# Third FFN stage: the up part is rounded by GpSimd, in place and with an added constant, instead of by ScalarE

## The chip, the cores and the metric

One core of one Trainium2 chip. The metric is the device time of one execution in microseconds, the median of the runs. Engines: TensorE (PE; PEld is its weight load), VectorE (DVE), ScalarE (ACT), GpSimd (POOL) and SyncE (SP), which only issues DMAs here.

## What is computed

Two layers of cross attention and FFN over x (4 x 1024 tokens, 256 wide), each with a residual. The change lies in the FFN of the first layer, which imitates 16-bit integers:

```python
def act_qdq(x):
    qmax = 2.0 ** (ACT_BITS - 1) - 1.0
    scale = jnp.maximum(jnp.max(jnp.abs(x)) / qmax, 1e-12)
    return jnp.clip(jnp.round(x / scale), -qmax - 1.0, qmax) * scale
x = act_qdq(x)
up = act_qdq(x @ lpbq_dequant(w_up).T)
gate = act_qdq(x @ lpbq_dequant(w_gate).T)
sig = fixed_qdq_u16(jax.nn.sigmoid(gate))
gate = act_qdq(gate * sig)
o = act_qdq(gate * up)
return o @ lpbq_dequant(w_down).T
```

Each act_qdq needs the largest absolute value of the whole tensor before it can round a single element. That is what cuts the FFN into stages.

## The kernel before

The program runs attention 0, the FFN, attention 1 and a mixture of experts one after the other. The function ffn is written as four blocks; between two blocks all engines meet. Inside a block each engine runs its own list of instructions in the order written, and counters (semaphores) hold it back.

The gate and the up part have 4096 x 768 values each. They are handled as NU = 24 units of 128 partitions x UW = 1024 columns. G holds all 24 units of the gate in SBUF; the up part has no room there and goes through DRAM (up_scratch), unit by unit.

The second block (lines 1690 to 1784) makes the up part and the gate times its sigmoid. In it GpSimd already runs two tensor_scalar per unit on f_sg (L1754, L1757: cap the sigmoid, then round it by adding GRID), and VectorE a scalar_tensor_tensor that takes GRID off and multiplies with an int16 tile (L1767), then two reduces (L1770, L1773). At its end SyncE issues the loads of the first four up units into ul[0..3] (L1504, called from load), and VectorE computes the scales ksl and kup, one value a partition, in SBUF.

The third block (from line 1786) is the one changed. Per unit u:

- ScalarE rounds the gate unit to int16, gq = round(G x ksl) (L1792), after product u-2 has freed that buffer (s_pr), and counts s_g3; then it waits for the load of the unit (s_ul) and rounds the up unit, uq = round(ul x kup) (L1794), and counts s_uq. gq and uq have two buffers each, ul has four.
- SyncE waits for s_uq of unit u-4 and issues the load of unit u into the same ul buffer (L1801, L1504).
- VectorE waits for s_g3 and s_uq, multiplies gq and uq into G (L1815) and counts s_pr; then it takes the largest absolute value of the unit before (L1819), one column of am3. These are products and reduces in the order product 0, product 1, reduce 0, product 2, reduce 1, and so on.
- TensorE only helps to spread the maximum over the partitions at the end (L1536, L1546). GpSimd has nothing to do.

After the last reduce, VectorE folds the 24 columns (L1823), the maximum is spread, and the fourth block starts: ScalarE rounds G again and TensorE multiplies with the down weights (L1882).

Of the kernel before, what the change touches and what calls it, by code (L numbers as in the profile page):

```python
# [9 lines left out]
I16 = mybir.dt.int16  # L10
U16 = mybir.dt.uint16
U8 = mybir.dt.uint8
ACT = mybir.ActivationFunctionType
AX = mybir.AxisListType
RMAX = bass.bass_isa.ReduceOp.max

P = 128
# [66 lines left out]
def pipeline(eng, body, first, last, lo, hi):  # L84

    for t in range(first, lo):
        body(At(t))
    with eng.Fori(0, (hi - lo + 1) // 2) as i:
        body(At(lo, i))
        body(At(lo + 1, i))  # L90
    for t in range(hi + 1, last + 1):
        body(At(t))
# [49 lines left out]
def _program(nc, stack, x, ctx_kv, mask, w, out):  # L142
# [32 lines left out]
    att0.close()  # L175
    old, sem = sem, Sems(nc)
    ffn(nc, sem, old, sbuf, xs, dict(fw, ident=ident, hmean=hmean, hrstd=hrstd, hamax=hamax, early=early))
    until_ffn.close()
    old, sem = sem, Sems(nc)
# [1223 lines left out]
def ffn(nc, sem, retired, sbuf, xs, c):  # L1403
# [12 lines left out]
    NU, UW = 24, 1024  # L1416
    UC = NU // NCH
    QM = 32767.0
    U16S = 65536.0
    GRID = 128.0  # L1420

    def s(n):
        return sem("f_" + n)
# [6 lines left out]
    s_ul, s_uq, s_g3, s_pr, s_am3 = [s(f"ul{i}") for i in range(4)], s("uq"), s("g3"), s("pr"), s("am3")  # L1430
# [4 lines left out]
    with ExitStack() as st:  # L1435
# [7 lines left out]
        am3 = sbuf(st, "am3", [P, NU])  # L1443
# [25 lines left out]
        r1, r2, r3 = Region(hold), Region(hold), Region(hold)  # L1469
# [8 lines left out]
        ul_at = r2.at  # L1478
        bh, bl = [[r2(f"f_b{v}{i}", [P, KT, CW], F32R) for i in range(2)] for v in "hl"]
        gq = [r3(f"f_gq{i}", [P, UW], I16) for i in range(2)]  # L1480
        uq = [r3(f"f_uq{i}", [P, UW], I16) for i in range(2)]
        assert r3.at <= ul_at
        r3.at = ul_at
        ul = [r3(f"f_ul{i}", [P, UW]) for i in range(4)]
# [5 lines left out]
        def unit(n):  # L1490
            return G[:, bass.ds(n * UW, UW)]
# [4 lines left out]
        def load_h(sp, t):  # L1496
            for i, h_ in enumerate((bh, bl)):
                sp.wait_ge(s_hs[t.p], t.of(lambda n: 32 * (n // 2 + 1)))
                sp.dma_start(h_[t.p][:].rearrange("p k n -> p (k n)").bitcast(F32),
                             hscr[bass.ds(t.n * 2 + i, 1)].rearrange("u p n -> p (u n)")  # L1500
                             ).then_inc(s_b[t.p], 16)

        def load(sp, t):
            sp.dma_start(ul[t.t0 % 4][:], uscr[bass.ds(t.n, 1)].rearrange("u p n -> p (u n)")  # L1504
                         ).then_inc(s_ul[t.t0 % 4], 16)
# [13 lines left out]
        def link(dve, instruction):  # L1519

            instruction.then_inc(s_sc, 1)
            links[0] += 1
            dve.wait_ge(s_sc, links[0])

        def integer_scale(dve, k, unit_scale, extra, scale, factor):

            dve.wait_ge(s_all, k + 1)
            link(dve, dve.tensor_scalar(tmp, ps[k % 2][:, 0:1], unit_scale, extra / QM, ALU.mult, ALU.mult))
            link(dve, dve.tensor_scalar(scale, tmp, 1e-12, None, ALU.max))
            link(dve, dve.reciprocal(tmp, scale))  # L1530
            link(dve, dve.tensor_scalar(factor, tmp, unit_scale, extra, ALU.mult, ALU.mult))

        def rows_max(pe, k):

            pe.wait_ge(s_loc, k + 1)
            pe.transpose(ps[6 + k % 2][0:1, 0:P], loc[:, k:k + 1], c["ident"][:]).then_inc(s_row, 1)  # L1536

        def fold_max(dve, k):
            dve.wait_ge(s_row, k + 1)
            dve.tensor_reduce(gmax[0:1, k:k + 1], ps[6 + k % 2][0:1, 0:P], AX.X, ALU.max).then_inc(s_gm, 1)  # L1540
            dve.wait_ge(s_gm, k + 1)
            dve.tensor_copy(grow[:, k % 2, :], gmax[0:1, k:k + 1].broadcast_to([1, P])).then_inc(s_bc, 1)

        def spread_max(pe, k):
            pe.wait_ge(s_bc, k + 1)
            pe.transpose(ps[k % 2][:, 0:1], grow[:, k % 2, :], c["ident"][0:1, 0:1]).then_inc(s_all, 1)  # L1546


        with nc.Block() as block:
            @block.sync  # L1550
            def _(sp):
                retired.clear(sp)

                def store(t):
                    for i, (h_, ready) in enumerate(((hh, s_hh), (hl, s_hl))):
                        sp.wait_ge(ready, t.of(lambda n: 2 * n + 2))
                        sp.dma_start(hscr[bass.ds(t.n * 2 + i, 1)].rearrange("u p n -> p (u n)"),
                                     h_[t.p][:].rearrange("p k n -> p (k n)").bitcast(F32)).then_inc(s_hs[t.p], 16)
                pipeline(sp, store, 0, NCH - 1, 2, 5)
                for i in range(2):  # L1560
                    load_h(sp, At(i))
                for i in range(2):
                    sp.wait_ge(s_hs[i], 32 * NCH // 2)
# [126 lines left out]
        with nc.Block() as block:  # L1690
# [58 lines left out]
            def _(pool):  # L1749
                def body(t):  # L1750
                    for q in range(UC):
# [4 lines left out]

                        pool.tensor_scalar(v, v, 1.0, GRID, ALU.mult, ALU.add).then_inc(s_su, 1)  # L1757
                for t in range(NCH):
# [3 lines left out]
            def _(dve):  # L1762
                def body(t):
                    for q in range(UC):
                        par = (t.t0 + q) % 2
                        dve.wait_ge(s_su, t.of(lambda n: UC * n + q + 1))
                        dve.scalar_tensor_tensor(unit(t.n * UC + q), sg[par][:], GRID, iq[q][:], ALU.subtract,  # L1767
                                                 ALU.mult).then_inc(s_g2, 1)
# [17 lines left out]
        with nc.Block() as block:  # L1786
            @block.scalar
            def _(act):
                def ints(t):
                    if t.t0 >= 2:  # L1790
                        act.wait_ge(s_pr, t.of(lambda n: n - 1))
                    act.activation(gq[t.p][:], unit(t.n), ACT.Copy, scale=ksl).then_inc(s_g3, 1)  # L1792
                    act.wait_ge(s_ul[t.t0 % 4], 16 * (t.t0 // 4 + 1))
                    act.activation(uq[t.p][:], ul[t.t0 % 4][:], ACT.Copy, scale=kup).then_inc(s_uq, 1)  # L1794
                for t in range(NU):
                    ints(At(t))

            @block.sync
            def _(sp):
                for t in range(4, NU):  # L1800
                    sp.wait_ge(s_uq, t - 3)  # L1801
                    load(sp, At(t))

            @block.tensor
            def _(pe):
                rows_max(pe, 4)
                spread_max(pe, 4)

            @block.vector
            def _(dve):  # L1810
                def body(t):
                    if t.t0 < NU:
                        dve.wait_ge(s_g3, t.of(lambda n: n + 1))
                        dve.wait_ge(s_uq, t.of(lambda n: n + 1))
                        dve.tensor_tensor(unit(t.n), gq[t.p][:], uq[t.p][:], ALU.mult).then_inc(s_pr, 1)  # L1815
                    a = t + -1
                    if a.t0 >= 0:
                        dve.wait_ge(s_pr, a.of(lambda n: n + 1))
                        dve.tensor_reduce(am3[:, bass.ds(a.n, 1)], unit(a.n), AX.X, ALU.max,  # L1819
                                          apply_absolute_value=True).then_inc(s_am3, 1)  # L1820
                pipeline(dve, body, 0, NU, 2, NU - 1)
                dve.wait_ge(s_am3, NU)
                dve.tensor_reduce(loc[:, 4:5], am3[:], AX.X, ALU.max).then_inc(s_loc, 1)  # L1823
                fold_max(dve, 4)
                link(dve, dve.tensor_tensor(sps, ssl, sup, ALU.mult))
                integer_scale(dve, 4, sps, 1.0, spr, kpr)
# [356 lines left out]
```

## Time and profile before

| | us |
|---|---|
| median of 3 runs (lowest, highest) | 1242.75 (1242.65, 1244.66) |
| profiled execution | 1243.19 |
| its span, first to last instruction | 1241.5 |
| third FFN block, first ScalarE operation to last reduce's end | 479.40 to 536.99 |
| busy share of TensorE, VectorE, ScalarE, GpSimd | 86%, 77%, 50%, 35% |

The span leaves out what lies around the instructions, 1.7 us here. In the timeline a row gives start, duration, engine, line, operation, output <- inputs; in brackets stands how long the engine was idle before it and who released it. The records of two VectorE operations in a row overlap by some 0.08 us, so the pace is read from their starts.

### The profile page before, as it was taken

Reading aid. Unit: us, or ns where it says so; the run is one execution under the profiler, and the core shown is the slowest. Engines: PE = TensorE matmul, PEld = TensorE weight load, DVE = VectorE, ACT = ScalarE, POOL = GpSimd, SP = SyncE. Lnnn points to the kernel's source line nnn. Section 1 sums busy time; section 2 is a strip of 40 time slices with the busy share of each in tenths; the row PEclk is TensorE's granted clock in tenths of the full one; section 3 lists DMA queues with packets and bytes.
Section 4 is the critical chain, followed back from the end, with each engine's and each line's share of the span. In section 5 each row is a group of like instructions: output and inputs, shape, how many; then the busy total and the mean of one; then the engine's idle time right before and its main releaser. Section 6 shows DMA issues by size and latency. Waiting matters only on the chain. (4 is left out here: it accounts for less than half of the span.)

```text
span 1241.5 us, 21565 instructions
## 1 busy us (share of the span) xinstructions
PE 1071.5 (86%) x6208; PEld 894.9 (72%) x6208; DVE 953.8 (77%) x2589; ACT 620.0 (50%) x1335; POOL 429.0 (35%) x514
## 2 busy tenths in 40 slices
PE   7999999996998980049986799999999969999998
PEld 5777777875886660049943698889888958777776
DVE  4688998885775998966453778887788758888886
ACT  1566777763556996967445233333333323332333
POOL 1245444441002881000011244455544533434333
PEclk9999999997999995569999899999999979999999
DMA  8000000000234766703123400101000000000000
GB/s 266 1 2 1 1 1 2 2 1 34 102 133 157 271 220 214 226 1 92 41 61 108 155 1 0 42 0 42 0 0 0 1 1 9 26 17 17 25 17 26
DMA packets 35551, 71.87 MB, mean 58 GB/s; under 512 B 3531, under 2 KB 23071, under 8 KB 35295
## 3 DMA queue, kind: packets, MB, share of 16 engines
q1 hardware_dynamic: 34111, 70.28, 17.0%
q10 hardware_dynamic: 1376, 0.79, 0.3%
q8 instruction: 33, 0.54, 0.2%
q14 instruction: 31, 0.25, 0.1%
HBM read 40.41 MB, written 30.65 MB: 57 GB/s over the span
## 5 line engine op out<-in xcount | busy, mean ns | idle before, releaser
L1068 PE MATMUL a_ps<-VW,a_PT 128*128 (+1 forms) x640 | 143.7, 380 | 0.0
L1068 PEld LDWEIGHTS a_ps<-VW,a_PT 128*128 128x128 f32 x640 | 119.5, 190 | 15.1
L1106 ACT ACTIVATE a_U<-a_U 128x1280 f32<-128x1280 f32 x32 | 40.7, 1270 | 112.5 <-DVE a_U L1179 112.5
L1085 ACT COPY a_PT<-a_ps 128x512 f32<-128x512 f32 (+1 forms) x96 | 46.0, 518 | 90.3 <-PE a_ps L1031 90.3
L1171 DVE TENSOR_REDUCE a_mx<-a_ps 128x4 f32<-128x320 f32 x128 | 62.3, 486 | 33.4 <-PE a_ps L1017 33.2
L1942 PE MATMUL m_ps<-m_wh,m_xh 128*128 128x512 f32 x256 | 87.1, 422 | 0.0
L2040 POOL TENSOR_TENSOR m_half<-m_half 128x512 f32<-128x512 f32 x32 | 41.0, 1283 | 132.3 <-ACT m_half L2002 132.3
L854 DVE TENSOR_SCALAR a_U<-a_ps 128x320 f32<-128x320 f32 x128 | 59.2, 483 | 32.9 <-PE a_ps L662 22.9
L1942 PE MATMUL m_ps<-m_wh,m_xl 128*128 128x512 f32 x256 | 82.1, 402 | 0.0
L1942 PE MATMUL m_ps<-m_wl,m_xh 128*128 128x512 f32 x256 | 81.4, 400 | 0.0
L745 PEld LDWEIGHTS a_ps<-vals,a_PT 128*128 128x128 f32 x640 | 76.4, 192 | 2.0 <-issue 0.4
L1017 PE MATMUL a_ps<-keysh,a_xnT 128*128 (+1 forms) x256 | 68.1, 347 | 10.8 <-DVE a_U L1179 9.3
L1123 POOL TENSOR_TENSOR a_U<-a_U,a_rc 128x1280 f32<-128x1280 f32 x32 | 74.6, 2332 | 7.3 <-DVE a_rc L1158 7.3
L745 PE MATMUL a_ps<-vals,a_PT 128*128 128x34 f32 (+1 forms) x640 | 74.2, 273 | 0.0
L2074 DVE SCALAR_TENSOR_TENSOR xs<-m_ps,m_g,xs 128x256 f32 (+1 forms) x128 | 61.2, 478 | 13.2 <-PE m_ps L1942 10.6
L2009 ACT ACTIVATE m_ex<-m_ls 128x8 f32<-128x8 f32 x32 | 6.7, 209 | 129.5 <-DVE m_ls L2095 129.5
L804 ACT ACTIVATE a_U<-a_U,a_mx 128x80 f32<-128x80 f32 x256 | 67.6, 346 | 0.0
L1536 PE MATMUL f_ps<-ident,loc 128*1 128x128 f32 x5 | 1.6, 362 | 75.4 <-DVE loc L1823 59.7
L1116 POOL TENSOR_TENSOR a_xrs<-a_xve,mhalf 128x1 f32<-128x1 f32 x32 | 17.5, 548 | 138.0 <-DVE a_xve L1227 138.0
L1754 POOL TENSOR_SCALAR f_sg<-f_sg 128x1024 f32<-128x1024 f32 x24 | 28.5, 1186 | 103.4 <-ACT f_sg L1718 103.3
L825 POOL TENSOR_TENSOR a_U<-a_U,a_mx 128x320 f32<-128x320 f32 x64 | 45.8, 718 | 46.4 <-DVE a_mx L859 46.0
L1179 DVE TENSOR_TENSOR a_U<-a_ps,a_mx 128x320 f32<-128x320 f32 x128 | 59.5, 486 | 2.2
(252 smaller groups left out, 3134.7 us busy)
## 6 DMA issues: line engine op xcount, KB each, us to landing
up_scratch<-f_ub SPq DMA_DIRECT2D x24, 512.0 KB, 2.9
f_ul<-up_scratch SPq DMA_DIRECT2D x24, 512.0 KB, 4.4
vw_scratch<-vw_stage SPq DMA_DIRECT2D x8, 640.0 KB, 4.2
VW<-vw_scratch SPq DMA_DIRECT2D x4, 1280.0 KB, 5.8
xs<-in_x SPq DMA_DIRECT2D x4, 1024.0 KB, 12.2
h_scratch<-f_hh SPq DMA_DIRECT2D x8, 512.0 KB, 2.6
h_scratch<-f_hl SPq DMA_DIRECT2D x8, 512.0 KB, 3.1
f_bh<-h_scratch SPq DMA_DIRECT2D x8, 512.0 KB, 4.5
```

The costliest lines, as they stand in the source:

```text
L745: last = pe.matmul(PV[:, h0 * E0:(h0 + nh) * E0], PTs[t.p][:, j, :], pr.vals[:].rearrange("p b s e -> p (b s e)")[:, bass.ds(t.batch * (NS ...
L804: last = act.activation(v, v, ACT.Exp, bias=mx[nxt.p][:, h:h + 1])
L825: pool.tensor_tensor(v, v, mx[a.p][:, 4 * g:4 * g + 4].unsqueeze(2).broadcast_to([P, 4, KP]), ALU.add).then_inc(s_sh, 1)
L854: dve.tensor_scalar(U[a.p][:, g * QW:(g + 1) * QW], S[sb[g]][:, 0:QW], CLAMP, -CLAMP, ALU.min, ALU.max).then_inc(s_clip, 1)
L1017: last = pe.matmul(S[sb[g]][:, 0:QW], x_[a.p][:, k, :], c[k_][:].rearrange("p b m n -> p (b m n)")[:, bass.ds(a.batch * (KT * SW) + k * SW ...
L1068: last = pe.matmul(Y[:, 0:D], PTs[t.p][:, j, :], c["VW"][:].rearrange("p b j d -> p (b j d)")[:, bass.ds(t.batch % 2 * (NJ * D) + j * D, D ...
L1085: act.copy(PTs[t.p][:, js[0]:js[-1] + 1, :].rearrange("p j n -> p (j n)"), R[k][:, 0:len(js) * P]).then_inc(s_PTe, 1)
L1123: pool.tensor_tensor(heads(U[a.p]), heads(U[a.p]), rc[a.p][:].unsqueeze(2).broadcast_to([P, H, KP]), ALU.mult).then_inc(s_N, 1)
L1171: dve.tensor_reduce(mx[a.p][:, 4 * g:4 * g + 4], quad(g), AX.X, ALU.max).then_inc(s_mx, 1)
L1179: dve.tensor_tensor(U[a.p][:, g * QW:(g + 1) * QW].rearrange("p (h k) -> p h k", k=KP), quad(g), mx[a.p][:, 4 * g:4 * g + 4].unsqueeze(2). ...
L1942: last = pe.matmul(o_, x_[a.p][:, k, :], w_[:, k, cols], start=(n == 0), stop=(n == 3 * KT - 1))
L2074: dve.scalar_tensor_tensor(xt(t), X[e // 2][:, (e % 2) * D:(e % 2 + 1) * D], g[t.p][:, e:e + 1], xt(t), ALU.mult, ALU.add).then_inc(s_acc, 1)
```

## The change

ScalarE's second operation and the tiles uq go. GpSimd gets a list of its own in the third block: as soon as a load has landed, it computes ul x kup + 12582912 in place. That number is 1.5 x 2^23; a float32 of that size has no fraction bits, so the sum is rounded to a whole number. VectorE's product becomes a scalar_tensor_tensor that subtracts the constant from ul and multiplies with gq. As ul is now read last by the product, the load that refills it waits for s_pr instead of s_uq. VectorE's loop over pairs of units is written out.

```diff
+    ROUND = 12582912.0
-        uq = [r3(f"f_uq{i}", [P, UW], I16) for i in range(2)]
@@ third block, scalar
-                def ints(t):
-                    if t.t0 >= 2:
-                        act.wait_ge(s_pr, t.of(lambda n: n - 1))
-                    act.activation(gq[t.p][:], unit(t.n), ACT.Copy, scale=ksl).then_inc(s_g3, 1)
-                    act.wait_ge(s_ul[t.t0 % 4], 16 * (t.t0 // 4 + 1))
-                    act.activation(uq[t.p][:], ul[t.t0 % 4][:], ACT.Copy, scale=kup).then_inc(s_uq, 1)
-                for t in range(NU):
-                    ints(At(t))
+                for u in range(NU):
+                    if u >= 2:
+                        act.wait_ge(s_pr, u - 1)
+                    act.activation(gq[u % 2][:], unit(u), ACT.Copy, scale=ksl).then_inc(s_g3, 1)
+
+            @block.gpsimd
+            def _(pool):
+                for u in range(NU):
+                    v = ul[u % 4][:]
+                    pool.wait_ge(s_ul[u % 4], 16 * (u // 4 + 1))
+                    pool.tensor_scalar(v, v, kup, ROUND, ALU.mult, ALU.add).then_inc(s_uq, 1)
 
             @block.sync
             def _(sp):
-                for t in range(4, NU):
-                    sp.wait_ge(s_uq, t - 3)
-                    load(sp, At(t))
+                for u in range(4, NU):
+                    sp.wait_ge(s_pr, u - 3)
+                    load(sp, At(u))
@@ vector
-                def body(t):
-                    if t.t0 < NU:
-                        dve.wait_ge(s_g3, t.of(lambda n: n + 1))
-                        dve.wait_ge(s_uq, t.of(lambda n: n + 1))
-                        dve.tensor_tensor(unit(t.n), gq[t.p][:], uq[t.p][:], ALU.mult).then_inc(s_pr, 1)
-                    a = t + -1
-                    if a.t0 >= 0:
-                        dve.wait_ge(s_pr, a.of(lambda n: n + 1))
-                        dve.tensor_reduce(am3[:, bass.ds(a.n, 1)], unit(a.n), AX.X, ALU.max,
-                                          apply_absolute_value=True).then_inc(s_am3, 1)
-                pipeline(dve, body, 0, NU, 2, NU - 1)
+                def largest(u):
+                    dve.wait_ge(s_pr, u + 1)
+                    dve.tensor_reduce(am3[:, u:u + 1], unit(u), AX.X, ALU.max,
+                                      apply_absolute_value=True).then_inc(s_am3, 1)
+
+                for u in range(NU):
+                    dve.wait_ge(s_g3, u + 1)
+                    dve.wait_ge(s_uq, u + 1)
+                    dve.scalar_tensor_tensor(unit(u), ul[u % 4][:], ROUND, gq[u % 2][:], ALU.subtract,
+                                             ALU.mult).then_inc(s_pr, 1)
+                    if u >= 1:
+                        largest(u - 1)
+                largest(NU - 1)
```

## Rows read from the trace of the kernel before

**Rows 1.** The page: the span in 40 slices, busy tenths of two engines.
```profile
DVE  4688998885775998966453778887788758888886
...
POOL 1245444441002881000011244455544533434333
```

**Rows 2.** Window of the third FFN stage: busy us of PE, PEld, DVE, ACT, POOL; clock, DMA.
```profile
489.00:495.00 6.00, 0.00 (x0) 0.00 (x0) 6.00 (x6) 5.98 (x6) 0.00 (x0) 0.50 0.81 249
```

**Rows 3.** Groups by line and form, 481 to 540 us: busy, mean ns | idle before.
```profile
L1794 ACT ACTIVATE f_uq<-f_ul,sc 128x1024 int16<-128x1024 f32 x24 | 27.2, 1132 | 0.0
```

**Rows 4.** Timeline of the stage's head: start, duration, engine, line, operation.
```profile
479.40 1.15 ACT L1792 ACTIVATE f_gq<-G,sc 128x1024 int16<-128x1024 f32 x1 [10.49 <-PEq L1690]
480.46 1.13 ACT L1794 ACTIVATE f_uq<-f_ul,sc 128x1024 int16<-128x1024 f32 x1
481.50 1.13 ACT L1792 ACTIVATE f_gq<-G,sc 128x1024 int16<-128x1024 f32 x1
481.62 6.56 SPq L1504 DMA_DIRECT2D f_ul<-up_scratch  x4
481.70 1.23 DVE L1815 TENSOR_TENSOR G<-f_gq,f_uq 128x1024 f32<-128x1024 int16 x1 [2.80 <-ACT f_uq L1794]
...
483.78 1.23 DVE L1815 TENSOR_TENSOR G<-f_gq,f_uq 128x1024 f32<-128x1024 int16 x1 [0.85 <-ACT f_uq L1794]
...
486.05 1.22 DVE L1815 TENSOR_TENSOR G<-f_gq,f_uq 128x1024 int16 x1
...
487.18 1.21 DVE L1819 TENSOR_REDUCE am<-G  x1
```

**Rows 5.** Timeline of the stage's end.
```profile
534.66 2.33 DVE L1819 TENSOR_REDUCE am<-G  x2
```

**Rows 6.** Timeline of the second FFN stage, its start.
```profile
388.65 1.04 POOL L1754 TENSOR_SCALAR f_sg<-f_sg 128x1024 f32<-128x1024 f32 x1 [90.44 <-ACT f_sg L1718]
...
389.78 1.06 POOL L1757 TENSOR_SCALAR f_sg<-f_sg 128x1024 f32<-128x1024 f32 x1
...
399.37 1.21 DVE L1767 SCALAR_TENSOR_TENSOR G<-f_sg,f_iq 128x1024 f32<-128x1024 f32 x1
...
400.50 1.21 DVE L1770 TENSOR_REDUCE amu<-f_ub 128x1 f32<-128x1024 f32 x1
```

**Rows 7.** Timeline of the second FFN stage, GpSimd and VectorE meeting.
```profile
412.97 1.23 DVE L1767 SCALAR_TENSOR_TENSOR G<-f_sg,f_iq 128x1024 f32 x1
413.05 2.04 POOL L1754 TENSOR_SCALAR f_sg<-f_sg 128x1024 f32<-128x1024 f32 x1 [0.26 <-ACT f_sg L1718]
...
414.11 1.21 DVE L1770 TENSOR_REDUCE amu<-f_ub 128x1024 f32 x1
...
416.30 1.04 POOL L1754 TENSOR_SCALAR f_sg<-f_sg 128x1024 f32<-128x1024 f32 x1
416.39 2.03 DVE L1767 SCALAR_TENSOR_TENSOR G<-f_sg,f_iq 128x1024 f32 x1
...
418.34 1.21 DVE L1770 TENSOR_REDUCE amu<-f_ub 128x1024 f32 x1
...
443.58 1.20 DVE L1773 TENSOR_REDUCE am<-G  x1
...
443.85 1.04 POOL L1754 TENSOR_SCALAR f_sg<-f_sg 128x1024 f32<-128x1024 f32 x1 [0.42 <-ACT f_sg L1718]
```

**Rows 8.** Groups by line: a two-input operation of GpSimd.
```profile
L2040 POOL TENSOR_TENSOR m_half<-m_half 128x512 f32<-128x512 f32 x32 | 41.0, 1283 | 132.3 <-ACT m_half L2002 132.3
```

**Rows 9.** The up loads, issue to landing: first four, next eight, last twelve.
```profile
L1504 SPq DMA_DIRECT2D f_ul<-up_scratch x4: 362/452/782, 469.4 to 471.1; - x4
...
DMA to landing us min/median/max: 4.6/6.1/7.0
...
DMA to landing us min/median/max: 3.5/4.2/4.4
...
DMA to landing us min/median/max: 4.0/4.4/4.5
```

## The prediction

> **What bounds the kernel now.** The page comes first: in the 17th of its 40 slices (496.6 to 527.6 us), wholly inside the third FFN stage and the only part the change touches, VectorE's digit is 9 and GpSimd's is 0 [rows 1]. The table of windows over that stage shows VectorE busy 6.00 of the 6 us from 489 to 495, ScalarE 5.98, GpSimd 0.00, and the DMA engines 0.81 [rows 2]. The reader is to see two engines that are both nearly full, and only one of them without a gap. One rounding of the up part takes ScalarE 1.13 us [rows 3], a product 1.22 and a reduce 1.21 us [rows 4]. VectorE's records overlap a little, so I take its pace from starts in the timeline: product 486.05, reduce 487.18, that is 1.13 us each and 2.26 us a unit [rows 4]. ScalarE, left alone, went from one gate rounding to the next in 2.10 us (479.40 to 481.50) [rows 4]. So VectorE bounds this stage from its second product (483.78) on, ScalarE only the head of it: product 0 waits until 481.70 for two roundings in a row, and product 1 sat idle 0.85 us for the next two [rows 4]. The last reduce ends at 536.99 [rows 5]. Check: 483.78 + 47 operations x 1.13 = 536.9.
>
> **What is removed.** 24 roundings of the up part on ScalarE, 24 x 1.13 = 27.2 us [rows 3]. They lie beside VectorE's work, so past the head their removal is worth nothing: VectorE is late next, and already was.
>
> **What stays as it is.** The product becomes a scalar_tensor_tensor with one float32 and one int16 input instead of two int16 inputs. The second stage has just that form (L1767): product 399.37, next operation 400.50, again 1.13 us [rows 6]. Cost 0.00 a unit, and below nothing it cannot go, since the reduces beside it show the same 1.13 us for 1024 columns [rows 4]. VectorE's loop becomes straight code; the loop's registers ran beside its work without a gap, so nothing. ScalarE's rounding of the gate now waits for product u-2 only; it has a whole cycle in hand.
>
> **What is added.** 24 tensor_scalar on GpSimd, in place, float32. The same shape with two immediate numbers takes 1.04 us when nothing hinders it (388.65, and 443.85) [rows 6, 7]. Here one of the two numbers is a column in SBUF (kup), and no GpSimd row shows that. The lower bound is 1.04; the upper one is a full second input: 1.28 us for 512 columns of two inputs makes up to 2.6 for 1024 [rows 8]. I take 1.04, because one value a partition is nearest to an immediate, and keep the upper half for a rival. At 1.04 in a cycle of 2.26 GpSimd itself is no bound.
>
> **What the two engines do to each other.** The second stage shows it in both directions. At 413.05 a GpSimd operation begins 0.08 us after a VectorE product; it lasts 2.04 instead of 1.04 and ends at 415.09, 0.98 us after VectorE's next operation began (414.11) [rows 7]. At 416.30 GpSimd is first by 0.09 us: the product of 416.39 lasts 2.03 instead of 1.21 and the next VectorE operation begins at 418.34, 1.00 us after GpSimd's end at 417.34, where an unhindered one comes 1.13 after its product's start [rows 7]. So a product held up behaves as if it had started 0.13 us before GpSimd ended, and GpSimd held up as if it started 0.06 us before the next VectorE operation. A reduce disturbs nobody: 443.58 reduce 1.20 us, 443.85 GpSimd 1.04 us, together [rows 7]. The product and GpSimd exclude each other, whoever is first; the reduce leaves 1.13 us in which GpSimd's 1.04 just fits.
> The Trainium skill ("SBUF — State Buffer", the list under its two sides of ports) has this as a rule that speaks against the change: GpSimd and a VectorE instruction with two SBUF inputs share one port pair as an exclusive lock, held for the whole instruction by whoever starts first. The trace agrees (2.04 and 2.03 us) [rows 7]. By the rule the head of the stage gains 0.4 us as below; without it, 2.0.
>
> **The head, step by step.** The stage's first ScalarE operation starts at 479.40 [rows 4]; GpSimd may start there too, since four loads were issued from 469.4 on and landed within 7.0 us at most [rows 9]. GpSimd unit 0: 479.40 to 480.44; unit 1 from 480.53 (0.09 later, as 388.65 + 1.04 to 389.78 [rows 6]) to 481.57. Product 0 wants to start at 480.66 (gate rounding to 480.55, plus the 0.11 seen from 481.59 to 481.70 [rows 4]), finds GpSimd 0.13 us ahead, and counts from 481.57 - 0.13 = 481.44. GpSimd unit 2 then gets the pair at 482.51 and ends at 483.55; product 1 counts from 483.42, reduce 0 comes at 484.55, product 2 at 485.68. Before, product 2 started at 486.05 [rows 4]. If product 1 went ahead of unit 2 instead, unit 3 would begin just ahead of product 2 and the same 485.68 would result. Gain: 486.05 - 485.68 = 0.37 us.
>
> **The loads, which are moved.** The refill of a slot was released by ScalarE's rounding of unit u and is now released by product u, its last reader; SyncE has nothing else queued. Steady, the refill goes out 1.21 + 0.03 = 1.24 us after the product's start (0.03: 481.59 to 481.62 [rows 4]), lands L later, and GpSimd starts, say, 0.11 after that, as VectorE did behind ScalarE [rows 4]. L was 4.0 to 4.5 us, median 4.4, for the last twelve loads and 3.5 to 4.4 for the eight before [rows 9]. GpSimd then ends 1.24 + 4.4 + 0.11 + 1.04 = 6.79 us after the product of four units earlier, against 4 x 2.26 = 9.04: the data are never late. But the end must also not fall past the start of the product of three units later by more than 0.13: with T for the cycle, 3T is at least L + 1.24 + 0.11 + 1.04 - 0.13 = L + 2.26. At L = 4.4, T = 2.22; at 4.5, 2.25; VectorE's 2.26 still decides, by a margin of 0.02 us in L (4.52). In other words GpSimd starts 1.1 to 1.3 us into the cycle, just behind the product.
>
> **Sum.** Span 1241.5 - 0.4 = 1241.1. The profiled execution took 1243.19, 1.7 outside the span, so 1242.8; it stood 0.4 above the median of 1242.75, hence 1242.4 us.
>
> **Rivals.**
> *A, slower: loads land later and GpSimd gets in front of the products.* Place: the reduce's slot, units 4 to 23. It decides from L = 4.52 us. At L = 5.0, T = 2.42, and 20 units x 0.16 = 3.2 us give 1245.6; at 5.5, T = 2.59 and 20 x 0.33 = 6.6 give 1249.0; past 5.52 the load lands behind the start of a product and the cost is gone. For it: the margin is 0.02 us, and the first four loads took 4.6 to 7.0 [rows 9]. Against it: those were issued within 2 us of each other, the spaced ones stayed at 4.5 or less, and a delay lengthens the cycle and so corrects two thirds of itself. Were there no such correction, each product could lose 2.03 - 1.21 = 0.82 us, 20 us in all. The Trainium skill ("GPSIMD Engine Reference", Key points) warns of just this, contention between GpSimd and VectorE instructions with two SBUF inputs; how often it strikes here no run shows yet. Chance 0.12.
> *B, slower: GpSimd pays for the scalar from SBUF.* Up to 1.3 us fits; at 1.9 a cycle is 1.9 + 1.13 - 0.06 - 0.13 = 2.84, and 23 units x 0.58 = 13 us give 1256. For it, only that no row shows the form. Chance 0.04.
> *C, faster by more than forecast: no blocking at the head.* Product 0 at 480.66, product 1 at 481.79, product 2 at 484.05 instead of 486.05: 2.0 us off, 1240.7. For it: GpSimd might begin a little late, so that product 0 comes first. Against: 416.30, where 0.09 us of lead decided [rows 7]. Chance 0.08.
> *D, the change does not do what it says:* GpSimd runs ahead at every unit and ScalarE was never the bound, so nothing moves: 1242.75. That is within my own case and not counted apart. Anything else, 0.02.
>
> **How the numbers follow.** My case, 1241.9 to 1243.5, has 0.74. A measurement of this kernel can tell about 0.2%, that is 2.5 us. Faster by more than that (under 1240.3) only the lucky end of C: 0.03. Slower (over 1245.2): A from L = 5.0 on, B and some of the rest, 0.13. Within: 0.84. The range: 1240.4 takes in C, 1247.0 takes in A up to about L = 5.2; B and the far end of A stay outside.
>
> **What would show it.** Product 2 at about 485.7 on the old time line; product starts 2.26 apart; GpSimd records starting 0.2 to 1.3 us after a product's start, lasting 1.04 to 2.0; product records of 1.21 to 1.27. Wrong would be: product records over 1.4 us again and again and starts 2.35 or more apart (A), GpSimd records that last over 1.3 us during a reduce (B), idle time of VectorE before products with a DMA or GpSimd named.

## The result, and the profile after

| | before | after |
|---|---|---|
| median, us | 1242.75 | 1240.13 |
| profiled execution; its span | 1243.19; 1241.5 | 1241.62; 1239.9 |
| third FFN block, first ScalarE operation to last reduce's end | 479.40 to 536.99 (57.59) | 480.62 to 538.22 (57.60) |
| mixture of experts, first to last record of its most frequent matmul line (L1942; after L1947) | 1019.1 to 1234.8 (215.7) | 1020.3 to 1233.2 (212.9) |

The ratio is 0.9979, interval 0.9970 to 0.9988: 2.6 us faster, 0.21%. Forecast were 1242.4 us and no measurable change; the range ended at 1240.4, so the time lies just below it. One of the 17 executions of after took 2728.09 us, in a slow state; the ratio leaves it out, and no trace of it was kept.

The table says where the time is. Everything ahead of the changed block, which the change doesn't touch, took 1.2 us longer in the profiled execution after. Single executions differ by that much and more: before ranged from 1239.91 to 1245.15 us. The changed block took as long as before. From its end to the mixture of experts both need 482.1 us, and from the start of the last matmul of L1942 (after: L1947) to the end of the span 6.7 us. The mixture of experts alone is 2.8 us shorter. 1.2 - 2.8 = -1.6, which is the difference of the spans. The whole gain lies in a stage that begins 482 us later and whose code the change leaves as it was, but for line numbers that are 5 higher.

The page after: two engines in 40 slices, as in [rows 1].

```profile
DVE  4798998884775999976554778888788758888886
...
POOL 1344445440002885410011245444554443334333
```

GpSimd's 17th slice has gone from 0 to 4, VectorE's stays 9 [rows 1]. The window of the changed stage, columns as in [rows 2]:

```profile
490.00:496.00 6.00, 0.00 (x0) 0.00 (x0) 6.00 (x7) 3.33 (x3) 3.91 (x3) 0.50 0.73 231
```

VectorE is as full as before, 6.00 of 6 us, ScalarE is down from 5.98 to 3.33. The groups of the stage after, columns as in [rows 3]:

```profile
L1799 POOL TENSOR_SCALAR f_ul<-f_ul,sc 128x1024 f32<-128x1024 f32 x24 | 31.0, 1293 | 29.4 <-DMA f_ul<-up_scratch 20.9 <-POOLq L1690 8.5
L1822 DVE SCALAR_TENSOR_TENSOR G<-f_ul,f_gq 128x1024 f32<-128x1024 f32 x24 | 30.9, 1292 | 1.8 <-POOL f_ul L1799 1.8
```

The head of the stage after, the timeline that answers to [rows 4]:

```profile
480.62 2.19 ACT L1792 ACTIVATE f_gq<-G,sc 128x1024 int16<-128x1024 f32 x2 [10.49 <-PEq L1690]
480.65 6.42 POOL L1799 TENSOR_SCALAR f_ul<-f_ul,sc 128x1024 f32<-128x1024 f32 x4 [8.45 <-POOLq L1690]
481.88 3.19 DVE L1822 SCALAR_TENSOR_TENSOR G<-f_ul,f_gq 128x1024 f32<-128x1024 f32 x2 [1.77 <-POOL f_ul L1799]
...
485.00 1.21 DVE L1816 TENSOR_REDUCE am<-G 128x1 f32<-128x1024 f32 x1
486.13 2.02 DVE L1822 SCALAR_TENSOR_TENSOR G<-f_ul,f_gq 128x1024 f32<-128x1024 f32 x1
...
488.07 1.21 DVE L1816 TENSOR_REDUCE am<-G 128x1 f32<-128x1024 f32 x1
```

GpSimd gets into its second unit ahead of product 0 and holds it back; product 1 follows at once, ahead of GpSimd's third unit (two products in 3.19 us), and product 2, held back by GpSimd's unit 3, lasts 2.02 us. Reduce 1 starts 7.45 us after the stage's first operation; before it was 487.18 - 479.40 = 7.78 [rows 4]. That is 0.33 us gained. It is lost again in the middle:

```profile
506.45 1.12 POOL L1799 TENSOR_SCALAR f_ul<-f_ul,sc 128x1024 f32<-128x1024 f32 x1 [1.37 <-DMA f_ul<-up_scratch]
507.29 1.35 DVE L1822 SCALAR_TENSOR_TENSOR G<-f_ul,f_gq 128x1024 f32<-128x1024 f32 x1
...
508.79 1.12 POOL L1799 TENSOR_SCALAR f_ul<-f_ul,sc 128x1024 f32<-128x1024 f32 x1 [1.22 <-DMA f_ul<-up_scratch]
509.69 1.29 DVE L1822 SCALAR_TENSOR_TENSOR G<-f_ul,f_gq 128x1024 f32<-128x1024 f32 x1
```

GpSimd's 506.45 operation starts when its load lands, 1.42 us into the cycle of 505.03, and ends 0.28 us into the product at 507.29, which then lasts 1.35 instead of 1.21 us. Four products of the stage have this (1.35, 1.29, 1.29, 1.25), and their cycles are 2.40, 2.34, 2.35 and 2.30 instead of 2.26: 0.14 + 0.08 + 0.09 + 0.04 = 0.35 us.

Then the mixture of experts. The chain of work that ended last there (start, us, what), of before:

```profile
1120.15 1.42 PE m_ps L1942 x6
...
1121.70 0.22 DVE m_ls L2095
...
1123.05 0.21 DVE m_sel L2112
...
1123.47 0.24 DVE m_g L2119
...
1124.13 0.44 DVE m_xl L2132
...
1124.61 0.61 PE m_ps L1970 x4
```

The same stretch of after:

```profile
1120.06 2.80 PE m_ps L1947 x12
1122.86 0.12 PE m_ps L2000
1122.98 1.41 PE m_ps L1947 x6
1124.39 0.50 PE m_ps L1975 x4
```

Before, the chain leaves TensorE for 3 us and runs through VectorE's routing of the experts, and so it does in each of the twelve turns; after, it never leaves TensorE. The fourth part of the page says the same in one line: PE 14%, DVE 2% and issue 1% of the span before, PE 17% and DVE 0% after. So here VectorE was on the path, by a small margin, with TensorE nearly full at the same time. Windows of 120 us inside this stage, columns as in [rows 2], first before, then after (TensorE has gone from 118.83 us to all 120.00, so little more is to be had here from VectorE):

```profile
1080.00:1200.00 120.00, 118.83 (x574) 95.09 (x573) 104.64 (x450) 40.24 (x144) 45.65 (x54) 1.00 0.06 20
```

```profile
1080.00:1200.00 120.00, 120.00 (x586) 96.80 (x584) 106.46 (x456) 41.11 (x144) 46.21 (x56) 1.00 0.06 20
```

The stage is a loop, and a turn handles two tiles of tokens. A turn, from one loop branch of VectorE to the next, took 13.38 us before and 13.17 after (medians of the 11 stretches between 12 branches). Where VectorE's turn got shorter is seen in its timeline at two places. Before:

```profile
1132.62 0.15 DVE L2152 TENSOR_SCALAR m_ve<-m_ag 128x1 f32<-128x1 f32 x1
1133.38 0.48 DVE L2074 SCALAR_TENSOR_TENSOR xs<-m_ps,m_g,xs 128x256 f32 x1 [0.60 <-PE m_ps L1942]
...
1136.40 0.23 DVE L2112 SCALAR_TENSOR_TENSOR m_sel<-m_iota,m_fi,m_sel 128x8 f32<-128x8 f32 x1
1136.85 0.23 DVE L2119 SCALAR_TENSOR_TENSOR m_g<-m_ex,m_rs,m_sel 128x8 f32<-128x8 f32 x1 [0.22 <-DVE m_sel L2112]
```

After:

```profile
1132.32 0.15 DVE L2157 TENSOR_SCALAR m_ve<-m_ag 128x1 f32<-128x1 f32 x1
1132.95 0.48 DVE L2079 SCALAR_TENSOR_TENSOR xs<-m_ps,m_g,xs 128x256 f32 x1 [0.48 <-PE m_ps L1947]
...
1135.97 0.23 DVE L2117 SCALAR_TENSOR_TENSOR m_sel<-m_iota,m_fi,m_sel 128x8 f32<-128x8 f32 x1
1136.32 0.23 DVE L2124 SCALAR_TENSOR_TENSOR m_g<-m_ex,m_rs,m_sel 128x8 f32<-128x8 f32 x1
```

Between the first two rows lies the loop's branch. From the start of the one to the start of the other it was 0.76 us, and is 0.63; I call it the way back. Between the other two lie only register and semaphore instructions: 0.45 us before, 0.35 after; I call it the halt. Together 1.21 and 0.98 us, and 0.23 is what a turn lost, within 0.02. From the first branch to the last it was 147.3 us before (1065.7 to 1213.0) and 144.8 after (1066.6 to 1211.4), 2.5 less. In the first turn, ahead of the first branch, the halt was 0.71 us before (1055.71 to 1056.42) and 0.35 after (1056.97 to 1057.32), 0.36 more. The two account for the stage's 2.8 us. The idle time of the way back is put down to TensorE in both, but nothing in TensorE's list changed between them. The sequencer's own records of the branch say more (first and last start us). Before:

```profile
L88 DVEq COMPARE_BRANCH  x1: 56/56/56, 1132.7 to 1132.7; - x1
L88 DVEq FUSED_REGOPS  x1: 63/63/63, 1133.0 to 1133.0; - x1
```

After:

```profile
L88 DVEq COMPARE_BRANCH  x1: 56/56/56, 1132.4 to 1132.4; - x1
L88 DVEq FUSED_REGOPS  x1: 63/63/63, 1132.6 to 1132.6; - x1
```

The branch itself takes 0.056 us in both; the loop's first instruction started 0.31 us after the branch did before, and 0.19 after. That instruction sets registers and waits for no semaphore, so no other engine can have held it up: the delay is in VectorE's own list of instructions.

### The profile page after: what moved, and what is told of

Its sections match the earlier page's. It is cut to its first block and busy times, and to the rows that moved or that the text cites. A ratio compares the mean times of both kernels' runs of the same rounds, so it can differ in the third digit from the quotient of the medians.

```text
span 1239.9 us, 21476 instructions
## 1 busy us (share of the span) xinstructions
PE 1070.6 (86%) x6208; PEld 895.1 (72%) x6208; DVE 959.2 (77%) x2589; ACT 596.8 (48%) x1311; POOL 459.6 (37%) x538
## 5 line engine op out<-in xcount | busy, mean ns | idle before, releaser
L1947 PE MATMUL m_ps<-m_wh,m_xh 128*128 128x512 f32 x256 | 87.2, 422 | 0.0
L1947 PE MATMUL m_ps<-m_wh,m_xl 128*128 128x512 f32 x256 | 82.0, 402 | 0.0
L1947 PE MATMUL m_ps<-m_wl,m_xh 128*128 128x512 f32 x256 | 81.4, 399 | 0.0
L745 PEld LDWEIGHTS a_ps<-vals,a_PT 128*128 128x128 f32 x640 | 79.5, 198 | 2.2 <-issue 0.4
L745 PE MATMUL a_ps<-vals,a_PT 128*128 128x34 f32 (+1 forms) x640 | 77.2, 279 | 0.0
L1116 POOL TENSOR_TENSOR a_xrs<-a_xve,mhalf 128x1 f32<-128x1 f32 x32 | 17.5, 548 | 135.5 <-DVE a_xve L1227 135.5
L817 POOL TENSOR_TENSOR a_xrs<-a_xve,mhalf 128x1 f32<-128x1 f32 x32 | 21.4, 669 | 114.3 <-DVE a_xve L928 114.3
```

Source lines behind the costliest of these rows:

```text
L745: last = pe.matmul(PV[:, h0 * E0:(h0 + nh) * E0], PTs[t.p][:, j, :], pr.vals[:].rearrange("p b s e -> p (b s e)")[:, bass.ds(t.batch * (NS ...
L1947: last = pe.matmul(o_, x_[a.p][:, k, :], w_[:, k, cols], start=(n == 0), stop=(n == 3 * KT - 1))
```

## The experiments

What could make a loop shorter whose code is unchanged? Either what the three engines do in the third block (ScalarE's list 24 instructions shorter, GpSimd's longer), or the removed loop of VectorE, or only where VectorE's instructions lie: writing the loop out makes VectorE's program 51 instructions longer ahead of the mixture of experts. Eleven kernels tell these apart, and a twelfth tests the rule for GpSimd. The first four do one thing each. The number 51 comes from the loop: its 14 instructions and one ahead of it did two units a turn, and written out the same 22 units take 66, 3 a unit. The expectation of e_unroll counts the loop's growth as 30 rows, and e_dve30 was made after that count, so it is not the same shift as e_unroll.

**e_unroll.** Before, with VectorE's loop of the third block written out, and nothing else.
```diff
-                pipeline(dve, body, 0, NU, 2, NU - 1)
+                for t in range(NU + 1):
+                    body(At(t))
```


> The kernel before with one part of the change: VectorE's loop of the third FFN stage written out, so that its program ahead of the mixture-of-experts loop is 30 rows longer (1586 instead of 1556 ahead of that loop's branch). Theory 1 (the gain of the changed kernel comes from where VectorE's code lies): about 1240.2 us, 2.6 below the kernel before, and 13.17 us instead of 13.38 for a pair of tiles in the mixture-of-experts loop; the third FFN stage stays at 57.6 us. Theory 2 (ScalarE's 24 fewer rows) and theory 3 (GpSimd's 26 more rows): 1242.7 and 13.38. Theory 4 (the gain lies in the third FFN stage after all): 1242.7.

Measured: 1239.35 us against 1242.02, ratio 0.9977 (0.9968 to 0.9986); a turn 13.17 us. This one edit gives all of the gain (0.9979). ScalarE's roundings are all there, GpSimd has nothing to do, and the third block takes 57.60 us (481.60 to 539.20), as in both other kernels.

**e_pool26.** Before, with 26 small GpSimd operations in the third block.
```diff
+            @block.gpsimd
+            def _(pool):
+                for i in range(26):
+                    pool.memset(amt[:, i:i + 1], 0.0)
```


> The kernel before with 26 one-column memsets added to GpSimd's list in the third FFN stage, where it has nothing to do. Theory 3 (GpSimd's longer program moves its later loops): about 1240.2 us and 13.17 us for a pair of tiles. Theories 1, 2 and 4: 1242.7 and 13.38.

Measured: 1242.27 us, ratio 1.0000 (0.9989 to 1.0011), a turn 13.38. The length of GpSimd's list has no part in it.

**e_act24.** After, with ScalarE's 24 instructions put back as copies of one column.
```diff
                     act.activation(gq[u % 2][:], unit(u), ACT.Copy, scale=ksl).then_inc(s_g3, 1)
+                    act.copy(sc[:, 13 + u % 8:14 + u % 8], sh)
```


> The changed kernel with 24 one-column copies added to ScalarE's list, one behind each gate rounding of the third FFN stage, where it then has about 1.1 us to spare; its program is as long again as in the kernel before. Theory 2 (ScalarE's shorter program): back to 1242.7 us and 13.38 us for a pair of tiles. Theories 1, 3 and 4: 1240.1 and 13.17; the third FFN stage itself stays at 57.6 us.

Measured: 1240.14 us, ratio to before 0.9980 (0.9968 to 0.9991), a turn 13.16. The gain stays with ScalarE's list as long as before, so its length has no part in it either.

**e_dve30.** Before, with 30 copies of one column at the head of VectorE's fourth block, where it waits for ScalarE anyway. This moves all that follows by 30 instructions and leaves the loop of the third block.
```diff
             def _(dve):
+                for i in range(30):
+                    dve.tensor_copy(amt[:, i:i + 1], sh)
+
                 def body(t):
```


> The kernel before with 30 one-column copies added to VectorE's list at the head of the fourth FFN stage, where it waits 2.8 us for ScalarE's first rounding; they write a scratch column each that nobody reads. Theory 1 (place of VectorE's code): about 1240.2 us and 13.17 us for a pair of tiles, as if the loop had been written out, or up to 0.5 more if the copies last longer than the wait. Theories 2, 3 and 4: 1242.7 and 13.38.

Measured: 1242.62 us against 1242.02, ratio 1.0003 (0.9994 to 1.0012), a turn 13.38. No gain, against what the expectation had for a mere shift. The copies were no cost that could hide it: they end ahead of the first product of the block.

```profile
536.47 2.12 DVE L1838 COPY amt<-sc 128x1 f32<-128x1 f32 x30 [0.52 <-PEq L1786]
538.78 1.22 DVE L1848 TENSOR_TENSOR wTl<-f_oq,wTh 128x1024 fp32r<-128x1024 int16 x1 [0.19 <-ACT wTh L1868]
```

Its timeline has something new, though. Same two places as above:

```profile
1129.00 0.15 DVE L2155 TENSOR_SCALAR m_ve<-m_ag 128x1 f32<-128x1 f32 x1
1129.85 0.48 DVE L2077 SCALAR_TENSOR_TENSOR xs<-m_ps,m_g,xs 128x256 f32 x1 [0.70 <-PE m_ps L1945]
...
1132.88 0.23 DVE L2115 SCALAR_TENSOR_TENSOR m_sel<-m_iota,m_fi,m_sel 128x8 f32<-128x8 f32 x1
1133.23 0.23 DVE L2122 SCALAR_TENSOR_TENSOR m_g<-m_ex,m_rs,m_sel 128x8 f32<-128x8 f32 x1
```

The halt is down to 0.35 us as in after, but the way back is 0.85 us instead of 0.76. The extra tenth hasn't gone; it has moved from the 32nd record of the loop's body to the 2nd, 30 places forward. So it doesn't seem to belong to an instruction, but to a place in VectorE's program.

**e_dve1, e_dve2, e_dve3 and e_aft1.** The same copies, one, two and three ahead of the unchanged loop, and one in after.

> The kernel before with one single one-column copy added at the head of VectorE's list for the fourth FFN stage, where it waits for ScalarE anyway. So far: writing the loop out makes VectorE's program 51 instructions longer and the mixture-of-experts loop faster, 30 more copies leave it as it was. Theory 1a (what counts is whether the loop ahead lies at an odd or an even place): about 1240 us, 13.16 us for a pair of tiles, and 0.19 instead of 0.31 us from the loop's branch to VectorE's next instruction. Theory 1b (a coarser grain than two instructions): some other value between 13.16 and 13.38, or 13.38. Theory 5 (not the place but the missing loop in the third FFN stage makes the later one faster): 1242.4 and 13.38.

> The same with two copies. Theory 1a: 13.38 us for a pair of tiles and 0.31 us behind the branch, as with none. Theory 1b: some other value. Theory 5: 13.38.

> The same with three copies, so that the place is as far from that of the kernel before as 51 is when counted in steps of four. Theory 1a: 13.16 us for a pair of tiles and 0.19 us behind the branch. Theory 1b with a grain of four: 13.16 here, and another value with one copy. Theory 5: 13.38.

> The changed kernel with one one-column copy added at the head of VectorE's list for the fourth FFN stage. Theory 1a: the gain is lost, 1242.5 us, 13.38 us for a pair of tiles and 0.31 us behind the branch, although all of the change is there. Theory 1b: between 1240.1 and 1242.5. Theory 5: 1240.1 and 13.16.

Measured: e_dve1 1244.46 us against 1243.81, ratio 1.0007 (0.9997 to 1.0017), a turn 13.33; e_dve2 13.33 and e_dve3 13.29 (one execution each, 1240.96 and 1241.08 us, so that only their turns are used); e_aft1 1239.71 us, ratio 0.9964 (0.9951 to 0.9978), a turn 13.17. Whether the shift is odd or even makes no difference, and three copies don't give what 51 give, so a step of four is out too. With one copy the halt is at the 31st record, with two at the 30th. With three copies the halt is down to 0.35 and the way back still 0.76. What is left of the theories: the way back is long as long as such a place lies inside the loop, and short once it has left the loop at its head, after some 32 instructions.

**e_dve36, e_dve51 and e_unroll13.** 36 and 51 copies ahead of the unchanged loop of before, and 13 copies on top of e_unroll, 64 in all.

> The kernel before with 36 one-column copies at the head of VectorE's list for the fourth FFN stage. A short halt inside the mixture-of-experts loop's first pass sat at VectorE's record 32 without padding, 31 with one copy, and near record 2 with thirty: it looks like an edge at a fixed place of VectorE's program over which the loop is shifted. Theory 6 (a loop's way back costs 0.31 us when such an edge lies in its first part, and 0.19 when not): 36 copies push the edge ahead of the loop, so 0.19 us behind the branch, about 13.16 us for a pair of tiles, and some 2.5 us off the total, 0.2 of it lost again because 36 copies last a little longer than the wait that hides them. Theory 5 (the missing loop in the third FFN stage is what counts, not the place): 0.31, 13.33 and the total of the kernel before.

> The same with 51 copies, so that the mixture-of-experts loop lies exactly where it lies with the third stage's loop written out. Theory 6: 0.19 us behind its branch and 13.16 us for a pair of tiles; attention 1's loop gets 0.27 instead of 0.19 us behind its branch, as in the changed kernel; the fourth stage begins up to 1.0 us late. Theory 5: 0.31 and 13.38, and 0.19 in attention 1.

> The kernel before with VectorE's loop of the third stage written out (51 instructions) and 13 one-column copies at the head of the fourth: 64 in all. Theory 6 with edges every 64 instructions: the halt is back at record 32, 0.31 us behind the branch, 13.38 us for a pair of tiles. Theory 6 with edges farther apart (128 or more), or theory 5: 0.19 and 13.16.

Measured: e_dve36 1239.47 us against 1242.26, ratio 0.9980 (0.9967 to 0.9992). That is the gain of the change from 36 useless instructions and nothing of the change. Its rows around the branch (the way back is 0.63 us; the halt's stretch is 0.34):

```profile
1129.45 0.15 DVE L2155 TENSOR_SCALAR m_ve<-m_ag 128x1 f32<-128x1 f32 x1
1130.08 0.48 DVE L2077 SCALAR_TENSOR_TENSOR xs<-m_ps,m_g,xs 128x256 f32 x1 [0.48 <-PE m_ps L1945]
```

That also rules out the missing loop as the cause, as the loop is there. e_dve51 and e_unroll13 ran once each (1240.81 and 1239.84 us); their turns are in the table. In e_unroll13 neither the halt nor the long way back has returned, against the first of the two theories in its expectation. All kernels by their shift, medians over the turns:

| VectorE instructions more than before | kernel | way back + halt, us | turn, us | attention 1, behind the branch, us |
|---|---|---|---|---|
| 0 | before, e_pool26 | 0.76 + 0.45 = 1.21 | 13.38 | 0.19 |
| 1 and 2 | e_dve1, e_dve2 | 0.76 + 0.41 = 1.17 | 13.33 | 0.19 |
| 3 | e_dve3 | 0.76 + 0.35 = 1.11 | 13.29 | 0.19 |
| 30 | e_dve30 | 0.86 + 0.35 = 1.21 | 13.38 | 0.19 |
| 36 | e_dve36 | 0.63 + 0.35 = 0.98 | 13.16 | 0.19 |
| 51 | e_dve51, e_unroll, after, e_act24, e_gpdelay | 0.63 + 0.35 = 0.98 | 13.16 to 13.17 | 0.27 |
| 52 | e_aft1 | 0.63 + 0.35 = 0.98 | 13.17 | 0.27 |
| 64 | e_unroll13 | 0.62 + 0.35 = 0.97 | 13.14 | 0.27 |

The turn less the two stretches is 12.16 to 12.19 us in every row: what VectorE saves there is what the stage saves. The last column is the same effect in another loop, VectorE's in attention 1, and goes the other way: at 51 and more its first instruction comes 0.27 us after the branch instead of 0.19. There a turn takes 19.27 to 19.28 us in all of them, so it costs nothing. e_dve51 keeps the loop of the third block and has the same pair of values as the four kernels in which it is written out; what they share is the number 51.

**e_gpdelay.** The other half of the prediction is the rule by which GpSimd gets in front of the products. After, with GpSimd held back by a memset (320 columns, 0.36 us) ahead of each rounding.
```diff
+                    pool.memset(gd[:], 0.0).then_inc(s_gd, 1)
+                    pool.wait_ge(s_gd, u + 1)
                     pool.tensor_scalar(v, v, kup, ROUND, ALU.mult, ALU.add).then_inc(s_uq, 1)
```


> The changed kernel with a 320-column memset of GpSimd (0.37 us) and a wait for it between each load's landing and the rounding, so that each rounding starts some 0.42 us later. If the prediction's rule for the third stage holds (three cycles are at least load time plus 1.24 + 0.08 + 1.12 - 0.13, here plus 0.42), a cycle takes (4.4 + 2.31 + 0.42) / 3 = 2.38 instead of 2.26 us, the stage 59.5 instead of 57.6 and the kernel 2 us more than the changed one. If GpSimd does not hold the products up, both stay as they are, as 0.42 us are small beside the two cycles of reserve that the data have.

Measured: 1243.83 us against 1242.26, ratio 1.0003 (0.9991 to 1.0015; the two medians alone would give 1.0013). By the ratios that is about 3 us more than after, which stands at 0.9979 to its own before. The third block takes 59.8 us (480.46 to 540.22) instead of 57.6, which is 2.2 of them; the rest is within the two intervals. The turn of the mixture of experts stays at 13.16. Its timeline:

```profile
491.24 0.36 POOL L1800 MEMSET f_gd<- 128x320 f32 x1
491.40 1.23 DVE L1825 SCALAR_TENSOR_TENSOR G<-f_ul,f_gq 128x1024 f32<-128x1024 f32 x1
491.69 1.91 POOL L1802 TENSOR_SCALAR f_ul<-f_ul,sc 128x1024 f32<-128x1024 f32 x1
492.54 1.21 DVE L1819 TENSOR_REDUCE am<-G 128x1 f32<-128x1024 f32 x1
...
493.71 1.23 DVE L1825 SCALAR_TENSOR_TENSOR G<-f_ul,f_gq 128x1024 f32<-128x1024 f32 x1
```

Products start 2.31 us apart. The stage's loss is near what was expected (2.2 against 1.9 us); the way to it is partly another. For the first dozen units the loads are no longer what times GpSimd: it starts 0.29 us behind a product, is held until that ends, lasts 1.91 us, and the next memset and the wait behind it bring the next rounding to 2.32 us after this one (491.69 and 494.01): its own chain is the cycle. Later single products are held too (one takes 2.10 us). So a GpSimd with 1.12 + 0.36 us of work a unit is already the bound of this stage, though that is far from filling the cycle of 2.26: a rounding that starts under a product is held until the product ends and takes 1.91 us.

## Why the prediction was wrong

**The head, a gain of 0.37 us.** Right: 0.33, with product 1 ahead of unit 2, which the prediction named as the other order with the same end. GpSimd's rounding takes 1.12 us (506.45), not the 1.04 of [rows 6]. That row caps the sigmoid; the one at 389.78, which multiplies and adds as the new one does, takes 1.06, so that 0.06 us are left for the scalar from SBUF. Rival B would have needed over 1.3.

**The product's new form, nothing.** Right: 1.21 us, and starts 2.26 or 2.27 us apart in 16 of the 20 cycles from 489.20 on.

**The exclusion of product and GpSimd.** Right (held products last 2.06 and 2.02 us, against 2.03 in [rows 7]), and so C, which needed its absence, did not occur: that the time is near C's 1240.7 is an accident.

**The loads and the rule 3T ≥ L + 2.26.** The mechanism was right, the size off by the same 0.08 us of the rounding and by loads whose times vary: with 1.12 the point from which it decides is L = 4.44 instead of 4.52, and the stage's loads have a median of 4.4 us. So it decided now and then, four times, for 0.35 us in all. The prediction gave rival A from L = 5.0 on, at 3.2 us; a tenth of that came. How often it decides differs between executions: e_aft1, with the same third block, has cycles of 2.30 us at most.

**The sum over the third block.** 0.33 gained and 0.35 lost is nothing, where 0.37 was forecast as gain. For this block it is rival D, that nothing moves, though for another reason.

**The step that failed** is the sentence "VectorE's loop becomes straight code; the loop's registers ran beside its work without a gap, so nothing". It is right for the loop that was written out, and it was asked of that loop alone. Writing it out made the program longer by 51 instructions and moved every later loop of VectorE. e_unroll shows that this by itself gives a ratio of 0.9977, against 0.9979 for the whole change, and e_dve36 (0.9980) that not even the loop has to go. The other mistake made this one possible: the views were read for the changed block alone. The chain of waits of before, read over the mixture of experts, passes through VectorE in every turn, and a tenth of a microsecond in it counts twelve times. With that chain in hand, a change that alters the number of VectorE's instructions is no longer safe to put at nothing, and 0.84 for no change was too much. But its size, some 2.8 us, is known from these runs alone. Nothing in the trace of before says on which side of such a place the loop would come to lie; before was at the slow end of the table, and from a kernel at its fast end the same edit could have led to the slow one.

**What is shown and what isn't.** Shown: the gain comes from the place of VectorE's instructions, and the two stretches account for it. Not shown: what kind of memory has its border at that place. The DMA queues that carry instructions, in the trace of before, 1050 to 1062 us:

```profile
q8 instruction: 1, 0.02, 0.5%
q14 instruction: 1, 0.01, 0.2%
```

The packet of q14 is worth a closer look. In before it falls into the window from 1057.6 to 1058.2 us, 1.3 us after VectorE's first pass over the record of the halt (1056.42), and it is the only one of q14 while the loop runs (1052.2 to 1213.0):

```profile
q14 instruction: 1, 0.01, 3.2%
```

In e_dve30 it falls into the window from 1050 to 1051 us, behind the second record of the first turn (the product after it starts at 1049.48):

```profile
q14 instruction: 1, 0.01, 1.9%
```

In e_dve36 it comes between 1049 and 1050 us and in after between 1049 and 1052, ahead of the loop, which they enter at 1050.7 and 1053.5. So the packet moves with the place: VectorE's first pass over it is followed by one packet of instructions. The packets of q14 are 8 KB each (31 with 0.25 MB in the page), and the place looks like the border of such a packet. That fits the table: a turn has 92 records of VectorE, and in e_unroll13 the place lies 32 ahead of the loop and no second one has come into it, so by an estimate from these numbers the next is over 120 instructions away.

But the slow turns don't wait for a packet. Between 1062 and 1222 us, with VectorE's turns of 13.38 us up to the last branch, neither queue has one; the only queue with any is q1:

```profile
q1 hardware_dynamic: 3264, 3.15, 5.8%
```

The Trainium skill ("Runtime: NRT & Kernel Launch", Instruction fetch mechanics) says that a taken branch whose target lies outside the two pages held forces a DMA fetch of the page. That fetch isn't what the slow turns here wait for. Why a pass over the place costs 0.10 us in every turn, and why the way back should grow by 0.12 us for as long as it lies within the loop, is open.

## What to carry to other kernels

Before an edit is priced at nothing because of what it does in its own stage, ask whether it changes the number of instructions of an engine that is on the chain anywhere later; if so, give its price an end for each turn of that loop, in either direction (here 0.22 us a turn; attention 1, whose way back moved by 0.08 us, lost nothing). When a measured gain is small and doesn't show in the changed stage, compare the turns of the later loops first, and put the same number of idle instructions into the old kernel before you credit the idea. The idea of this change, GpSimd's rounding in place, is worth 0 here: it relieves an engine that wasn't the bound.

## What the runs showed of the hardware

- Behind a loop's branch VectorE's first instruction came after 0.19 or 0.31 us in the mixture of experts (0.18 in e_unroll13), and after 0.19 or 0.27 in attention 1, with the same code, by its place in the program. The branch's own record takes 0.056 us in all.
- A place in VectorE's program at which it halts for 0.10 us moves through the code one for one with inserted instructions (32nd record to 31st, 30th and 2nd, with 1, 2 and 30 inserted). Its first pass is followed by one 8 KB packet of the instruction queue q14, about 1 us later. Under other waits part of it hides (one or two copies leave 0.06, three nothing).
- A tensor_scalar of GpSimd on 1024 float32 columns takes 1.12 us with one scalar a partition from SBUF (multiply, add), 1.06 with two immediates (multiply, add) and 1.04 with two immediates (minimum, maximum).
- An idle time's releaser can be wrong for such halts: TensorE was named for the way back, but the 0.12 us between the fast and the slow one came with VectorE's own next instruction.
